# First cross attention of a perceiver kernel: key weights folded into the queries, probabilities turned by VectorE, weighted sums in bursts of 32x32 tiles

## The reference

```python
# x (1,128,256), ctx (1,12544,256); 16 heads, D_K = 64, D_V_HEAD = 16
q = (layernorm(x) @ wq).reshape(B, 128, 16, 64).transpose(0, 2, 1, 3)
k = (ctx @ wk).reshape(B, 12544, 16, 64).transpose(0, 2, 1, 3)
v = (ctx @ wv).reshape(B, 12544, 16, 16).transpose(0, 2, 1, 3)
attn = softmax(einsum('bhqd,bhkd->bhqk', q, k) / sqrt(64))
x = x + einsum('bhqk,bhkd->bhqd', attn, v)      # heads side by side again
```

## Time and profile before

| what | value |
|---|---|
| runs | 1283.72, 1285.89, 1286.67 us |
| profiled execution | 1286.79 us, its span 1284.8 us |
| PE busy | 1209.5 us (94%) |
| DVE, ACT busy | 876.3 us (68%), 768.9 us (60%) |
| POOL busy | 11.0 us (1%) |
| mean granted TensorE clock | 0.972 |
| first attention, from its first scores to `x0_read` | 33.3 to 902.1 us |

### The profile page before, as it was taken

How to read it: one execution, slowest core, us unless ns; L and a number is a source line. 1 busy time by engine, 2 the same in 40 slices (tenths; PEclk the granted TensorE clock), 3 DMA queues, 4 the chain that set the end, 5 groups by cost and what they waited for, 6 DMA issues and landing times.

```text
span 1284.8 us, 22961 instructions
## 1 busy us (share of the span) xinstructions
PE 1209.5 (94%) x9518; PEld 976.9 (76%) x9518; DVE 876.3 (68%) x1471; ACT 768.9 (60%) x1470; POOL 11.0 (1%) x39
## 2 busy tenths in 40 slices
PE   5799999999999999999999999998588999769999
PEld 4577777777777777777777777776477888658998
DVE  5688888888888888888888888886512555243222
ACT  5577777777777777777777777776222555221111
POOL 1000000000000000000000000000000000010000
PEclk9799999999999999999999999999788999889999
DMA  3500000000000000000000000000913334802883
GB/s 102 206 17 16 2 17 16 16 16 16 16 16 16 16 16 16 1 15 16 16 16 16 16 16 0 1 2 1 346 55 131 98 117 144 289 1 67 303 290 132
DMA packets 53244, 83.99 MB, mean 65 GB/s; under 512 B 2624, under 2 KB 37712, under 8 KB 53200
## 3 DMA queue, kind: packets, MB, share of 16 engines
q1 hardware_dynamic: 52384, 82.05, 19.1%
q10 hardware_dynamic: 816, 1.31, 0.3%
HBM read 83.23 MB, written 0.13 MB: 65 GB/s over the span
## 4 chain that ended last, share of the span: by engine, by line
PE 89%; DVE 4%; ACT 3%; issue 2%; DMA 1%; POOL 0%; SPq 0%; DVEq 0%; POOLq 0%; PEldq 0%
PE ps L399 16%; PE ps L353 8%; PE ps L317 7%; PE ps L321 7%; PE ps L319 7%; PE ps L346 7%; PE ps L347 7%; PE ps L1295 5%; PE ps L1307 5%; PE ps L914 3%; PE ps L820 2%; PE ps L329 2%; PE ps L328 2%; PE ps L330 2%; PE ps L895 2%
## 5 line engine op out<-in xcount | busy, mean ns | idle before, releaser
L552 DVE TENSOR_TENSOR keys<-ps,keys 64x512 fp32r<-64x512 f32 (+1 forms) x400 | 271.1, 678 | 72.1 <-ACT keys L461 67.0
L461 ACT CAST keys<-ps 64x512 fp32r<-64x512 f32 (+1 forms) x400 | 228.6, 572 | 104.3 <-PE ps L321 94.4
L569 DVE TENSOR_REDUCE negc<-ps 128x2 f32<-128x1024 f32 (+1 forms) x200 | 239.6, 1198 | 57.9 <-PE ps L347 57.0
L479 ACT ACTIVATE probs<-ps,negm 128x512 f32<-128x512 f32 (+1 forms) x400 | 250.7, 683 | 2.3 <-DVE negm L572 2.3
L399 PE MATMUL ps<-ident,probs 128*128 128x128 f32 x1568 | 219.1, 282 | 3.5 <-ACT probs L479 1.9
L399 PEld LDWEIGHTS ps<-ident,probs 128*128 128x128 f32 x1568 | 166.6, 141 | 48.5 <-issue 38.1
L498 ACT COPY probsT<-ps 128x512 f32<-128x512 f32 (+1 forms) x200 | 115.6, 578 | 120.0 <-PE ps L399 119.9
L346 PE MATMUL ps<-keys,q_hi 128*128 128x512 f32 (+1 forms) x400 | 173.7, 435 | 3.8 <-issue 2.3
L317 PE MATMUL ps<-ctxT_hi,wk_hi 128*128 128x512 f32 (+1 forms) x400 | 162.5, 406 | 11.7 <-DVE keys L552 7.1
L321 PE MATMUL ps<-ctxT_hi,wk_lo 128*128 128x512 f32 (+1 forms) x400 | 157.5, 394 | 0.0
L347 PE MATMUL ps<-keys,q_lo 128*128 128x512 f32 (+1 forms) x400 | 157.2, 393 | 0.0
(11 more groups left out here) (232 smaller groups left out, 1430.0 us busy)
## 6 DMA issues: line engine op xcount, KB each, us to landing
m_w<-in_m_w SPq DMA_DIRECT2D x32, 1024.0 KB, 7.5
ctx_raw<-in_ctxT SPq DMA_DIRECT2D x24, 512.0 KB, 3.6
ctx_one<-in_ctx SPq DMA_DIRECT2D x24, 512.0 KB, 4.1
f_h1T<-in_f_h1T SPq DMA_DIRECT2D x1, 4096.0 KB, 12.8
f_h2T<-in_f_h2T SPq DMA_DIRECT2D x1, 4096.0 KB, 22.4
m_shared_w<-in_m_sw SPq DMA_DIRECT2D x2, 1024.0 KB, 9.1
x_wk<-in_x_wk ACTq DMA_DIRECT2D x2, 512.0 KB, 5.9
x_wq<-in_x_wq SPq DMA_DIRECT2D x2, 512.0 KB, 8.5
```

What stands on the lines that cost most here:

```text
L461: act.copy(m.keys[half, 2 * p + j, cols], bank[half, cols]).then_inc(s["k_hi"], 1)
L479: t = act.activation(m.probs[p % 2][:, j, 0:nt * P], m.ps[:, 2 * (p % 2) + j, 0:nt * P], ACT.Exp, bias=m.negm[slot][:, 2 * p + j:2 * p + j ...
L552: t = dv.tensor_tensor(m.keys[other, 2 * p + j, cols], bank[half, cols], m.keys[half, 2 * p + j, cols], ALU.subtract)
L569: dv.tensor_reduce(m.negc[:, cols], m.ps[:, 2 * (p % 2):2 * (p % 2) + 2, 0:nt * P], AX.X, ALU.max).then_inc(s["dve"], 1)
```

## The change

The scores of a head are q·(Wk c), which is also (Wk q)·c. The changed kernel multiplies the key weights into the queries once (`folded_queries`), and then takes scores straight from the context, whose width is 256 instead of 64. No keys are computed. The 16 heads x 128 queries are laid out anew: in step `t` the 128 output rows hold 32 queries (block `t % 4`) of four heads, and two such groups `c` are taken at once, so that there are again eight steps with 1024 columns in two banks. A step's scores are now twelve products of 512 columns.

The rows of probabilities are turned by VectorE in blocks of 32x32 (`turn_probabilities`) into `probsT`, which holds a whole chunk. TensorE's 64 transposes for each chunk and the copies behind them go. The weighted sums of a chunk are done in one burst in step 1 of the next chunk (`weighted_sums`): 256 fp32 products of 32 rows by 32 columns by 128, each at one of 16 tile positions in the array; row group `j` writes bank `4 + j`. Values are computed transposed, twice six products of 512 columns in steps 3 and 5, and turned by VectorE too. GpSimd takes over the context's low part and the update of `acc`; for that, `alpha` is laid out again by 16 small transfers for each chunk on SyncE's queue. The result goes through 16 more small transfers (`outputs_sync`). Since the buffers now lie over the place of `w1`, `w2` and `w3`, these 3 MiB are loaded after `x0_read`, ahead of and behind `h1T` and `h2T`, and all of them ahead of the 16 small ones.

```diff
-        for p in range(PAIRS):            # xattn0_tensor.chunk: scores, key_products, value_products,
-            ...                           # weighted and 2 x 4 transposes, as above
+    def folded_queries(k, c):
+        for j in range(4):
+            p, rows = 4 * (c // 2) + j, (TOP, LOW)[c % 2]
+            i = pe.matmul(m.bank(FOLD_BANKS[QUADS * k + c])[:, j * P:(j + 1) * P], m.wkT[rows, p, k * P:(k + 1) * P],
+                          m.qT[rows, p, :], start=True, stop=True)
+        i.then_inc(s["fold_full"], 1)
+    def scores(slot, t, nt):
+        cols, qb = slice(0, nt * P), t % 4
+        for odd in range(2):
+            c = 2 * (t // 4) + odd
+            dst = m.bank(2 * (t % 2) + odd)[:, cols]
+            for k in range(DK):
+                pe.matmul(dst, m.qk_hi[:, k, c, qb, :], m.c_hi[slot][:, k, cols], start=(k == 0), stop=False)
+                pe.matmul(dst, m.qk_hi[:, k, c, qb, :], m.c_lo[slot][:, k, cols], start=False, stop=False)
+                i = pe.matmul(dst, m.qk_lo[:, k, c, qb, :], m.c_hi[slot][:, k, cols], start=False, stop=(k == DK - 1))
+        i.then_inc(s["scores_full"], 1)
+    def weighted_sums(slot, nt):
+        for b in range(4 * nt):
+            for j in range(4):
+                for c in range(QUADS):
+                    i = pe.matmul(m.ps[32 * c:32 * (c + 1), 4 + j, 0:P], m.vals[slot][32 * j:32 * (j + 1), b, c, :],
+                                  m.probsT[slot][32 * j:32 * (j + 1), c, b, :], start=(b == 0),
+                                  stop=(b == 4 * nt - 1), tile_position=(32 * j, 32 * c), skip_group_check=True)
+        i.then_inc(s["out_full"], 1)
+        for t in range(STEPS):            # xattn0_tensor.chunk
+            after = step_after(slot, t, nt, ahead)
+            if after:
+                ...
+                if nt_before or t:
+                    pe.wait_ge(s["scores_read"], n("scores_read"))
+                scores(*after)
+            if nt_before and t == SUM_STEP:
+                pe.wait_ge(s["v_kept"], n("v_kept", 2))
+                pe.wait_ge(s["probs_turned"], n("probs_turned"))
+                weighted_sums(1 - slot, nt_before)
+            ...
+            if t in VALUE_STEPS:
+                value_products(slot, VALUE_STEPS.index(t), nt)
+    def exponentials(slot, t, nt):        # ScalarE
+        act.wait_ge(s["max_ready"], n("max_ready"))
+        for odd in range(2):
+            i = act.activation(m.probs[t % 2][:, odd, 0:nt * P], m.ps[:, 2 * (t % 2) + odd, 0:nt * P], ACT.Exp,
+                               bias=m.negm[slot][:, 2 * (t // 4) + odd, t % 4:t % 4 + 1], scale=1.0)
+        i.then_inc(s["probs_ready"], 1)
+        act.drain().then_inc(s["scores_read"], 1)
+    def turn_probabilities(slot, t, nt):  # VectorE
+        dv.wait_ge(s["probs_ready"], n("probs_ready"))
+        cs = slice(2 * (t // 4), 2 * (t // 4) + 2)
+        i = dv.transpose(m.probsT[slot][:, cs, 0:4 * nt, t % 4 * 32:t % 4 * 32 + 32],
+                         m.probs[t % 2][:, :, 0:nt * P].rearrange("p c (b k) -> p c b k", k=32))
+        ...
+        for t in range(STEPS):            # xattn0_vector.chunk
+            after = step_after(slot, t, nt, ahead)
+            if after:
+                maxima(*after)
+            turn_probabilities(slot, t, nt)
+            if nt_before and t == SUM_STEP:
+                if added:
+                    dv.wait_ge(s["acc_added"], n("acc_added"))
+                turn_out()
+            if t in VALUE_STEPS:
+                turn_values(slot, VALUE_STEPS.index(t), nt)
+def place_alpha(sp, m, s, n, slot):
+    sp.wait_ge(s["alpha_ready"], n("alpha_ready"))
+    for j in range(4):
+        for c in range(QUADS):
+            sp.dma_start(m.alphaT[slot][32 * c:32 * (c + 1), j, :],
+                         m.alpha[slot][32 * j:32 * (j + 1), c, :]).then_inc(s[f"alpha_placed{slot}"], 16)
 def layer0_sync(sp, m, s, n, a):
     sp.wait_ge(s["x0_read"], 1)
+    sp.dma_start(m.w1T[:, :, :], a["f_w1T"].rearrange("(k p) n -> p k n", p=P)).then_inc(s["f_up"], 16)
+    sp.dma_start(m.w2T[:, :, :], a["f_w2T"].rearrange("(k p) n -> p k n", p=P)).then_inc(s["f_up"], 16)
     sp.dma_start(m.h1T[:, :, :], a["f_h1T"].rearrange("(k p) n -> p k n", p=P)).then_inc(s["f_h1"], 16)
     sp.dma_start(m.h2T[:, :, :], a["f_h2T"].rearrange("(k p) n -> p k n", p=P)).then_inc(s["f_h2"], 16)
+    sp.dma_start(m.w3T[:, :, :], a["f_w3T"].rearrange("(k p) n -> p k n", p=P)).then_inc(s["f_down"], 16)
+    outputs_sync(sp, m, s)
```

More of the change, by code:

```diff
@@ L340, in queries @@
         t.then_inc(s["q_full"], 1)
[L342 to L351, removed]
-            for j in range(4):
[L353 to L362, removed]
-    def chunk(slot, nt, nt_before, ahead):
-        for p in range(PAIRS):
[L366 to L373, removed]
-                pe.wait_ge(s["k_kept"], n("k_kept"))
-                if ahead > 1 and p == FREE_STEP:
+    def folded_queries(k, c):
[4 more added lines that the diff above has]
+        i.then_inc(s["fold_full"], 1)
@@ new lines, in xattn0_tensor @@
+    pe.wait_ge(s["ident"], 1)
+    layer_norm_tensor(pe, m, s, n, 3)
+    pe.wait_ge(s["xnT_ready"], n("xnT_ready"))
+    for half in range(2):
+        queries(half)
+    pe.wait_ge(s["wkT"], 16)
+    for c in range(QUADS):
+        if c % 2 == 0:
+            pe.wait_ge(s["q_ready"], n("q_ready"))
+        if c == QUADS - 1:
+            pe.wait_ge(s["q_ready"], 2)
+        for k in range(DK):
+            folded_queries(k, c)
+    pe.wait_ge(s["ctx_split"], n("ctx_split", 2))
+    pe.sem_inc(s["raw_free"], 1)
@@ new lines, in exponentials, with chunk @@
+    def exponentials(slot, t, nt):
+        act.wait_ge(s["max_ready"], n("max_ready"))
+        for odd in range(2):
[3 more added lines that the diff above has]
+        act.drain().then_inc(s["scores_read"], 1)
+    def chunk(slot, nt, ahead):
+        for t in range(STEPS):
+            exponentials(slot, t, nt)
+            if t == STEPS - 1:
+                act.activation(m.alpha[slot][:, :, :], m.dm[:, :, :], ACT.Exp).then_inc(s["alpha_ready"], 1)
+            if ahead and t in SPLIT_STEPS:
+                split_context(1 - slot, SPLIT_STEPS.index(t), CHUNK_TILES)
@@ L519, in xattn0_scalar @@
[L519 to L527 removed]
+    chunk(0, TAIL_TILES, 1)
+    chunk(1, CHUNK_TILES, 1)
+    looped = ("raw0", "raw1", "max_ready")
     n.restart(act, s, *looped)
[L529 to L531 removed]
+    with act.Fori(0, (N_FULL - 2) // 2):
+        chunk(0, CHUNK_TILES, 1)
+        chunk(1, CHUNK_TILES, 1)
@@ L603, in xattn0_vector, with chunk @@
+    def chunk(slot, nt, nt_before, ahead, added=True):
+        for t in range(STEPS):
+            after = step_after(slot, t, nt, ahead)
[8 more added lines that the diff above has]
+                turn_values(slot, VALUE_STEPS.index(t), nt)
     dv.wait_ge(s["x"], 16)
@@ new lines, in xattn0_vector @@
+    dv.wait_ge(s["wv_hi"], n("wv_hi"))
+    dv.tensor_tensor(m.wv_lo[:, :, :], m.wv[:, :, :], m.wv_hi[:, :, :], ALU.subtract).then_inc(s["wv_split"], 1)
+    dv.wait_ge(s["x0_init"], 1)
+    maxima(0, 0, TAIL_TILES)
+    chunk(0, TAIL_TILES, 0, 1)
+    chunk(1, CHUNK_TILES, TAIL_TILES, 1, added=False)
+    looped = ("scores_full", "dve", "probs_ready", "v_full", "out_full", "acc_added")
+    n.restart(dv, s, *looped)
+    with dv.Fori(0, (N_FULL - 2) // 2):
+        chunk(0, CHUNK_TILES, CHUNK_TILES, 1)
+        chunk(1, CHUNK_TILES, CHUNK_TILES, 1)
+        n.restart(dv, s, *looped)
@@ new lines, in xattn0_vector @@
+    chunk(0, CHUNK_TILES, CHUNK_TILES, 0)
+    dv.wait_ge(s["acc_added"], n("acc_added"))
+    turn_out()
+    dv.wait_ge(s["acc_added"], n("acc_added"))
+    dv.reciprocal(m.den[:, :, :], m.acc[:, :, :, X0_DV]).then_inc(s["dve"], 1)
+    dv.wait_ge(s["dve"], n("dve"))
+    dv.tensor_tensor(m.y0[:, :, :, :], m.acc[:, :, :, 0:X0_DV], along(m.den[:, :, :], X0_DV),
+                     ALU.mult).then_inc(s["y_ready"], 1)
+    dv.wait_ge(s["y_placed"], 256)
+    dv.tensor_tensor(m.x[1][:, :], m.x[0][:, :], m.yx[:, :], ALU.add).then_inc(s["dve"], 1)
```

452 lines of the change are left out of this document (162 added, 290 removed).

## The result

The changed kernel takes 1410.84 us (four runs, 1409.36 to 1414.84) against 1286.28 for the kernel before: 1.098 times as long, 95% interval 1.095 to 1.101. The forecast was 1192, faster, within 1155 to 1300. The profiled execution of after has a span of 1412.4 us.

A forecast was written before the change was run, and what follows sets the result against it. TensorE, busy 94% of the span, was taken to bound the kernel. Opening -7.8, tail and first full chunk -30.0, other 23 chunks -87.6, stage's end +29.5, slow-clock start +1: -94.9 from 1286.8 gives 1192 us, range 1155 to 1300.

The forecast's parts named there:

- 1.28 us each: TensorE's instruction queue: 32 packets at 0.2% of 16 x 1284.8 us, taken as the price of fetching one packet.
- W: Time of one chunk's burst of 256 small products, 512 records: taken as 5.0 us, ends 3.7 and 13.9.
- TensorE waits for its program: TensorE's longer loop isn't kept; each pass fetches 9.6 packets, 12.4 us if nothing hides it: 1328 us; chance 0.07.
- The half way of the first rival: In the burst, two positions in one column each wait for their second record: 7.1 us a burst, 1243 us; chance 0.08.
- Rival one: In the burst at most four positions work at a time: 13.9 us instead of 5.0, so 1410 us; chance 0.12.
- Scores without the burst: A full chunk's scores and values on TensorE, burst left aside: 25.5 us, between 24.9 and 26.1.
- VectorE's transpose: VectorE's turn of 1024 elements per partition in each step: 1.22 us, upper end 2.4, hidden at 1.22.
- the second rival: VectorE's transpose in each step costs double, about 4 us a chunk more: 1290 us; chance 0.08.
- Opening: Start of the stage, with queries and folding: first scores at 25.5 us instead of 33.3, so -7.8 us.
- Tail and first full chunk: The tail's eight steps and values, then the next chunk with half a burst: 43.6 us against 73.6, so -30.0.
- End: End of the stage: result copies cross SyncE's queue behind 11 MiB of weights, +29.5 us.
- the overtaking copies: At the stage's end the result copies overtake the weights, costing 2 us instead of 29.5: 1164 us; chance 0.10.

The follow-up runs named there:

- the kept one: The changed kernel with the burst of weighted sums left out in every second chunk of the loop, half the result missing: 1202.6 us.
- wider small ones: The changed kernel with 128 products of 32 x 64 by 256 columns in place of 256 of 32 x 32 by 128: 1261.4 us.
- the 32-record piece: The changed kernel with each burst cut into 16 pieces of 16 products, one behind every three score products of steps 1 to 4: 1324.1 us.

## Why the prediction was wrong

- **The step that failed** is the one that valued the fetches: "1.28 us each" and "more likely most of it hides behind products of 0.23 us, and only the burst's four packets, 5.1 us, bound W". The 1.28 was the time that a packet's transfer occupies the DMA engines, not the time from asking to having it. In the burst the packets come 3.4 to 4.3 us apart, so a burst is 12.5 us where the kept one is 6.9: +5.6 a chunk. The rival "TensorE waits for its program" was the right mechanism at a third of its price and a chance of 0.07. Its pass fetched 9.6 packets, the trace has 12. "Most of it hides behind products of 0.23 us" held: between long products the fetches are hidden (1269 against 1411), and behind wider small ones too (1263 against 1261).
- **The slow clock** that follows the gaps was in no term: +1.1 us a chunk (27.1 against 26.0 in the run without gaps, and 33.0 - 7.16 = 25.8 with the wider products).
- **W itself** was 6.9, not 5.0: I carried four starts 7 ns apart over to 512. They hold for the first 32 records, one round of the sixteen positions; then one comes each 13 ns. +1.9 a chunk. The half way of the first rival, 7.1, is near the kept burst's 6.9; its mechanism, two positions in a column taking turns, doesn't fit a first round with no such pause.
- **Rival one gave 1410 and was wrong.** Records on sixteen positions are under way at once: 32 begin within 0.23 us and each lasts 0.27. A time that agrees proves no mechanism: the gaps in L361 told them apart.
- **Scores without the burst:** 26.0 us against 25.5, near. Together 5.6 + 1.1 + 1.9 + 0.5 = 9.1, which is 39.6 - 30.5; 22 chunks of it are 200 of the 219 us of error. The last chunk has two bursts and 21 us more than I gave it; opening and end nearly cancel.
- **VectorE's transpose** was right: 1.22 taken, 1.24 measured, the second rival falls.

```profile
L491 DVE STREAM_TRANSPOSE probsT<-probs 128x1024 f32<-128x1024 f32 x160 | 197.8, 1236 | 0.0
```

- **Opening:** first scores at 22.58 us, forecast 25.5. **Tail and first full chunk:** the loop begins at 68.6, 46.0 later, forecast 43.6.
- **End:** +31.3 us (34.7 against 3.4), forecast 29.5. The direction and cause held: the weights took 30.2 us (996.8 to 1027.0, forecast 31.4), and the copies overtook nothing. The last copy landed 4.5 us behind them, forecast 1.5: two issues had held SyncE for 9.8 us each, and the other fifteen took 10.
- **The range's low end** doesn't follow from its own terms: the overtaking copies and a burst at its floor are 1192 - 27.5 - 24.5 x 1.3 = 1133, not 1155. It changes nothing here.
- The Trainium skill, "TensorE: Matmul & The Clock Gate", "Wait — 56ns, not 53.3ns?": its 25 ns between starts would have given, as an estimate, about 12.8 us a burst. The kept burst has 13 ns and the 32-record piece 7 ns, so the measurement stands against that floor across positions. The Trainium skill, "Runtime: NRT & Kernel Launch", "Instruction fetch mechanics", says that crossing a block is mostly hidden and that TensorE holds 2048 instructions. The first holds in the runs whose 256 instructions last 3.6 us or more, and not in the burst with 1.7. Of the second the traces show less as far as loops go: 1,854 were not kept.

## What to carry to other kernels

Count a loop's instructions as well as its work: when a change makes it denser, ask whether the pass is still kept (here seven packets were, eight weren't) and whether 256 instructions hold enough work (here 3.6 us was enough, 1.7 wasn't); if not, fewer and larger instructions can win even at twice the arithmetic, and so can the same ones in pieces between long products. Price a fetch by its latency, from asking to having, not by the share its queue shows. Small result copies go ahead of bulk loads: here neither the same queue nor another let them past.

## What was not expected of the hardware

- In after, each burst, with its gaps of 0.65 to 2.4 us, was followed or overlapped by 1.2 GHz for 6.8 to 13.7 us in the loop (0.50 between 244 and 252, above), while in the kept loop 512 small products without a gap kept 2.4 GHz.
- The branch of a loop that wasn't kept took a median of 3.4 to 3.8 us against 0.21.
- A change between whole-array products and 32-row ones cost some 0.4 us both ways together.
- Sixteen positions took 13 ns a record over a whole burst, but 7 ns in the first round, before any position came back.
- A DMA's issue, 0.6 us for a small copy otherwise, held SyncE for 9.8 us twice behind 10 and 11 MiB of weights.
